# Attention on one core: the negated row maxima enter the transposed logits as a repeated stationary column times a unit matrix, and the values are split on ScalarE and VectorE

## The reference

```python
q, k, v = qkv(x)                                   # per image: 12 heads, 196 tokens, 16 channels
attn = einsum('bqd,bkd->bqk', q * scale, k)        # 196 x 196 per head
attn = attn + rel_h[..., :, None] + rel_w[..., None, :]   # bias from the query and the key's row and column
attn = softmax(attn, axis=-1)
out = einsum('bqk,bkd->bqd', attn, v) @ proj_w + proj_b
```

## Time and profile before

| | |
|---|---|
| three runs | 1793.18 us median (1792.56 to 1794.38) |
| the profiled execution, first to last instruction | span 1796.6 us |
| TensorE busy | 1485.9 us, 83% |
| VectorE busy | 1269.7 us, 71% |
| ScalarE busy | 973.4 us, 54% |
| GpSimd busy | 855.0 us, 48% |
| first layer's loop, reduce of step 0 to that of step 95 | 642.83 to 895.89 us |
| second layer's loop | 1483.92 to 1737.07 us |
| GpSimd busy in 850 to 900 us; in 1650 to 1700 us | 49.62 of 50; 49.48 of 50 |
| ScalarE's copy of the maxima (L1316), mean of 192 | 490 ns |
| granted TensorE clock, 700 to 900 us | 1.00 (full, 2.4 GHz) |

### The profile page before, as it was taken

One profiled execution on the slowest core, in us unless ns is written; L12 is line 12 of the kernel. 1 busy time (PEld: TensorE's weight loads), 2 busy tenths in 40 slices (PEclk: granted clock), 3 DMA queues, 4 the chain that ended last, 5 costly groups with the idle time before them and its releaser, 6 DMA issues. The chain is left out here.

```text
span 1796.6 us, 51708 instructions
## 1 busy us (share of the span) xinstructions
PE 1485.9 (83%) x19315; PEld 1272.1 (71%) x19315; DVE 1269.7 (71%) x4444; ACT 973.4 (54%) x1990; POOL 855.0 (48%) x1080
## 2 busy tenths in 40 slices
PE   4868888888876888889977999899998697888978
PEld 4757777777765776767755667678774586777766
DVE  7877787877778567879956684544446646888974
ACT  3633333333344567889924234555543556888972
POOL 2712222222235056879952111456551416787984
PEclk9955555555558889999986589899995798999998
DMA  3000000000002596667215204322225468666712
GB/s 87 1 20 4 4 5 4 4 4 4 4 3 83 171 257 151 147 156 161 58 48 173 98 24 151 125 81 86 83 73 153 144 159 254 166 147 150 146 29 58
DMA packets 72178, 165.21 MB, mean 92 GB/s; under 512 B 17938, under 2 KB 43162, under 8 KB 69436
## 3 DMA queue, kind: packets, MB, share of 16 engines
q1 hardware_dynamic: 66556, 149.05, 31.3%
q0 software_dynamic: 5376, 12.85, 2.3%
HBM read 93.84 MB, written 67.42 MB: 90 GB/s over the span
## 5 line engine op out<-in xcount | busy, mean ns | idle before, releaser
L1080 POOL TENSOR_TENSOR l_arena<-l_arena,l_arena 98x784 fp32r<-98x784 f32 x192 | 358.4, 1872 | 91.3 <-ACT l_arena L1328 79.0
L514 PE MATMUL gru_ps_r<-gru_hp,gru_wp 128*128 128x16 f16 x3920 | 200.1, 176 | 68.1 <-DVE gru_hp L489 68.1
L514 PEld LDWEIGHTS gru_ps_r<-gru_hp,gru_wp 128*128 128x128 f16 x3920 | 150.8, 106 | 88.5 <-DVE gru_hp L489 88.5
L567 POOL TENSOR_TENSOR gru_kept<-gru_keep,l0s_state 128x32 f32<-128x32 f32 x196 | 49.3, 251 | 305.4 <-ACT gru_keep L582 305.4
L1388 DVE TENSOR_REDUCE l_ps<-l_ps 98x4 f32<-98x784 f32 x192 | 187.5, 977 | 9.1 <-PE l_ps L1159 3.2
L514 PE MATMUL gru_ps_n<-gru_hp,gru_wp 128*128 128x16 f16 x3920 | 191.1, 174 | 0.0
L1197 PE MATMUL l_ps<-l_arena,l_arena 128*66 128x196 f32 x768 | 162.1, 264 | 20.9 <-POOL l_arena L1080 20.1
L580 ACT ACTIVATE gru_reset<-gru_ps_r,gru_unscale 128x32 f32<-128x32 f32 x196 | 56.4, 288 | 216.8 <-PE gru_ps_r L514 216.8
L1325 ACT ACTIVATE l_arena<-l_ps 98x784 fp32r<-98x784 f32 x192 | 158.4, 825 | 4.6
L1328 ACT ACTIVATE l_arena<-l_ps 98x784 f32<-98x784 f32 x192 | 157.0, 818 | 0.0
L1198 PE MATMUL l_ps<-l_arena,l_arena 128*66 128x196 f32 x768 | 155.0, 255 | 0.0
(11 more groups left out here) (389 smaller groups left out, 4568.9 us busy)
## 6 DMA issues: line engine op xcount, KB each, us to landing
l_arena<-qk SPq DMA_DIRECT2D x96, 294.0 KB
qk<-l_arena SPq DMA_DIRECT2D x48, 392.0 KB, 9.0
rel<-l_arena SPq DMA_DIRECT2D x24, 686.0 KB
l_arena<-rel SPq DMA_DIRECT2D x48, 343.0 KB
qk<-l_arena SPq DMA_DIRECT2D x12, 784.0 KB, 7.9
l_arena<-in_experts_dram SPq DMA_DIRECT2D x8, 1152.0 KB, 7.6
l_arena<-x SPq DMA_DIRECT2D x24, 294.0 KB, 5.3
l_arena<-x SPq DMA_DIRECT2D x24, 196.0 KB, 3.1
```

Source lines behind the costliest of these rows:

```text
L514: last = pe.matmul(out[:, b, B * m:B * m + B], wp[:, wi, g, m, :], hp[:, b, part, B * k:B * k + B], start=False, stop=True, skip_group_che ...
L1080: pool.tensor_tensor(pl[g % LOWS][:TH, :, :], p32[:TH, g % 2, :, :], ph[:TH, g % 4, :, :].bitcast(f32), ALU.subtract).then_inc(pl_ready, 1)
```

## The change

The maxima are no longer made into rows. VectorE's reduce writes the **negated** maxima straight into an SBUF tile `mt`, in one instruction. TensorE multiplies a stationary operand that is one column of `mt` repeated 98 times with a unit matrix repeated twice; the result, which has the negated maximum of each query in every row, is added in PSUM onto the transposed logits. I call these 4 matmuls **M**. X, its copy on ScalarE and the splitting of the maxima on VectorE are gone, as are the two rows in `q` and `k` and the fourth piece of each load. The splitting of the values leaves GpSimd: ScalarE rounds (`round_values`) after its exponentials, VectorE subtracts (`lower_values`) between its reduce and its keep, each in two of every four steps, and the first two groups ahead of the loop.

```diff
-ROWS = 106
-Q_ROWS, REL_ROWS = 2, 50
+ROWS = 104
+Q_ROWS, REL_ROWS = 0, 48
...
-    LOADS, SLOTS, LOWS = 4, 3, 3
+    LOADS, SLOTS, LOWS = 3, 3, 3
...
-        mt, ones_at = s.sb("mt", [128, 4, 2], bf16), s.sb("ones_at", [128, TH], bf16)
+        mt, unit = s.sb("mt", [128, 2, 4], f32r), s.sb("unit", [128, TH], f32r)
...
-                def split_values(n):
...
                 def logits_by_key(g):
                     b = g % B
-                    pe.wait_ge(x_copied, g + 1)
                     if g >= 2:
                         pe.wait_ge(p_ready, g - 1)
                     queries = slice(b * T, (b + 1) * T)
+                    both = unit[:TH, :].rearrange("p (a t) -> p a t", a=1).to_broadcast([TH, 2, TH])
                     for head in range(2):
+                        bank = ps[:TH, T_BANK + 2 * (g % 2) + head, :TB]
                         for half in range(2):
                             keys = slice(b * T + half * TH, b * T + (half + 1) * TH)
-                            last = pe.matmul(ps[:TH, T_BANK + 2 * (g % 2) + head, half * T:half * T + T], k[:, head, keys],
-                                             q[:, head, queries], start=True, stop=True)
+                            pe.matmul(bank[:, half * T:half * T + T], k[:, head, keys], q[:, head, queries],
+                                      start=half == 0, stop=False, skip_group_check=True)
+                    pe.wait_ge(max_ready, g + 1)
+                    for head in range(2):
+                        bank = ps[:TH, T_BANK + 2 * (g % 2) + head, :TB].rearrange("p (k t) -> p k t", k=2)
+                        for half in range(2):
+                            n = 2 * head + half
+                            last = pe.matmul(bank[:, :, half * TH:(half + 1) * TH], mt[:TH, g % 2, n:n + 1].to_broadcast([TH, TH]), both,
+                                             start=False, stop=half == 1, skip_group_check=True)
                     last.then_inc(t_summed, 1)
...
-                    if 1 <= i <= IMAGES:
-                        b = (i - 1) % B
-                        act.wait_ge(x_ready, i)
-                        act.activation(q[0:2, :, b * T:(b + 1) * T], ps[64:66, R_BANK, :TB].rearrange("p (h t) -> p h t", h=2), ACT.Copy).then_inc(x_copied, 1)
...
                         act.activation(p32[:TH, g % 2, :, :], banks, ACT.Exp).then_inc(p_ready, 1)
+                        n = g // 4 + 1
+                        if g >= 6 and n < IMAGES // 4 and g % 4 in (2, 3):
+                            act.wait_ge(o_summed, 4 * n - 4)
+                            round_values(n, g % 4 - 2)
...
+                def lower_values(n, head):
+                    dve.wait_ge(vh_ready, 2 * n + head + 1)
+                    dve.tensor_tensor(value_parts(n, head, 1), values_of(n, head), value_parts(n, head, 0).bitcast(f32), ALU.subtract).then_inc(vl_ready, 1)
...
                         dve.wait_ge(s_summed, i + 1)
-                        m = ps[:TH, S_BANK, 400:404]
-                        dve.tensor_reduce(m, ps[:TH, S_BANK:S_BANK + 2, :TB].rearrange("p c (h k) -> p c h k", h=2),
-                                          AXIS.X, ALU.max).then_inc(mx_ready, 1)
-                        dve.wait_ge(mx_ready, i + 1)
-                        if i >= 1:
-                            dve.wait_ge(x_ready, i)
-                        dve.tensor_copy(mt[:TH, :, 0], m).then_inc(mh_ready, 1)
-                        dve.wait_ge(mh_ready, i + 1)
-                        dve.tensor_tensor(mt[:TH, :, 1], m, mt[:TH, :, 0], ALU.subtract).then_inc(ml_ready, 1)
+                        if i >= 2:
+                            dve.wait_ge(t_summed, i - 1)
+                        dve.tensor_reduce(mt[:TH, i % 2, :], ps[:TH, S_BANK:S_BANK + 2, :TB].rearrange("p c (h k) -> p c h k", h=2),
+                                          AXIS.X, ALU.max, negate=True).then_inc(max_ready, 1)
+                    n = i // 4
+                    if 8 <= i < IMAGES and i % 4 in (2, 3):
+                        lower_values(n, i % 4 - 2)
```

More of the change, by code:

```diff
@@ L926, in load @@
                     rel = rel_dram[quad].rearrange("(g h r) c n -> g r c h n", g=2, h=2)[at].rearrange("r c h n -> (r c) h n")
-                    dst, row, src = ((q, Q_ROWS, qk[0]), (k, Q_ROWS, qk[1]), (q, REL_ROWS, rel), (q, 0, k[ROWS:ROWS + 2]))[piece]
-                    rows = 2 if piece == 3 else src.shape[0]
+                    dst, row, src = ((q, Q_ROWS, qk[0]), (k, Q_ROWS, qk[1]), (q, REL_ROWS, rel))[piece]
+                    rows = src.shape[0]
                     sp.dma_start(dst[row:row + rows, :, cols].bitcast(f32), src[:, :, cols].bitcast(f32)).then_inc(quarter_in[part], 16)
@@ L956, in main_step @@
                     p, b = divmod(i, B)
-                    part, piece = divmod(b - EACH - 1, LOADS)
-                    if i < IMAGES and p + 1 < PAIRS and part >= 0:
+                    part, piece = divmod(b - EACH - 1, EACH)
+                    if i < IMAGES and p + 1 < PAIRS and part >= 0 and piece < LOADS:
                         load(p + 1, part, piece)
-                    if i < IMAGES and p > 0 and part < 0:
-                        load(p, (b + B - EACH - 1) // LOADS, (b + B - EACH - 1) % LOADS)
+                    if i < IMAGES and p > 0 and part < 0 and piece < LOADS:
+                        load(p, part + PARTS, piece)
                     if i % 5 == 3 and i < 50:
@@ L1034, in _ @@
                 pool.wait_ge(q_padded, 1)
-                def split_values(n):
-                    p, part = divmod(n, 4)
-                    halves, slots = slice(8 * part, 8 * part + 8), slice(n % 2 * 8, n % 2 * 8 + 8)
-                    def whole(head):
-                        return v[:TH, halves, 32 * p + HD * head:32 * p + HD * head + HD]
-                    def place(head, low):
-                        at = 32 * head + HD * low
-                        return vs[:TH, slots, head, at:at + HD]
-                    def high(head):
-                        pool.tensor_copy(place(head, 0), whole(head)).then_inc(vh_ready, 1)
-                    def low(head):
-                        pool.wait_ge(vh_ready, 2 * n + head + 1)
-                        pool.tensor_tensor(place(head, 1), whole(head), place(head, 0).bitcast(f32), ALU.subtract).then_inc(vl_ready, 1)
-                    return high, low
                 def split_reciprocals(h):
@@ L1069, in _ @@
                 pool.wait_ge(pl_padded, LOWS)
-                for n in range(2):
-                    high, low = split_values(n)
-                    for head in range(2):
-                        high(head)
-                    for head in range(2):
-                        low(head)
                 for g in range(IMAGES):
@@ L1161, in logits_by_query @@
                     last.then_inc(s_summed, 1)
-                def maxima_to_rows(g):
-                    pe.wait_ge(ml_ready, g + 1)
-                    if g >= 1:
-                        pe.wait_ge(x_copied, g)
-                    for n in range(4):
-                        last = pe.matmul(ps[64:66, R_BANK, n * TH:n * TH + TH], mt[:TH, n, :], ones_at[:TH, :], start=True, stop=True)
-                    last.then_inc(x_ready, 1)
                 def logits_by_key(g):
                     b = g % B
-                    pe.wait_ge(x_copied, g + 1)
                     if g >= 2:
@@ L1299, in constants @@
                     act.wait_ge(const_in, 16)
-                    act.activation(ones_at[:TH, :], ident[:TH, :], ACT.Copy).then_inc(ident_ready, 1)
+                    act.activation(unit[:TH, :], ident[:TH, :], ACT.Copy).then_inc(ident_ready, 1)
                     act.wait_ge(pick_in, 16)
@@ L1311, in _, with round_values @@
                 last_order(item, value)
+                def round_values(n, head):
+                    act.activation(value_parts(n, head, 0), values_of(n, head), ACT.Copy).then_inc(vh_ready, 1)
+                act.wait_ge(ones_ready, 2)
+                for n in range(2):
+                    for head in range(2):
+                        round_values(n, head)
                 for i in range(IMAGES + 2):
-                    if 1 <= i <= IMAGES:
-                        b = (i - 1) % B
-                        act.wait_ge(x_ready, i)
-                        act.activation(q[0:2, :, b * T:(b + 1) * T], ps[64:66, R_BANK, :TB].rearrange("p (h t) -> p h t", h=2), ACT.Copy).then_inc(x_copied, 1)
                     if i >= 2:
@@ L1383, in _ @@
                 last_order(item, lambda i: None)
+                def lower_values(n, head):
+                    dve.wait_ge(vh_ready, 2 * n + head + 1)
+                    dve.tensor_tensor(value_parts(n, head, 1), values_of(n, head), value_parts(n, head, 0).bitcast(f32), ALU.subtract).then_inc(vl_ready, 1)
+                for n in range(2):
+                    for head in range(2):
+                        lower_values(n, head)
                 for i in range(IMAGES + LAG):
```

27 lines of the change are left out of this document (11 added, 16 removed).

## The result

The changed kernel takes **1782.43 us** (median of 9 runs, 1777.34 to 1790.41) where the kernel before takes 1792.56 (median of 9 beside it, 1784.84 to 1796.63). The ratio is 0.9946, with a 95% interval of 0.9928 to 0.9964: faster by 0.5%, about 10 us. The profiled execution of the changed kernel has a span of 1779.3 us.

The account below looks back on a forecast made before the run. GpSimd bounds A steps, VectorE's table-piece ring B and C steps. Per layer 4.1 (A) - 1.5 (C) - 1.4 (B) + 1.4 (ends) = 2.6 us, 5.2 for both: 1788 us, range 1772 to 1822.

Parts of the forecast that it names:

- the side that was given 0.47: Whole kernel: faster by over 0.2%, the summed forecast at 0.30 plus the rival without exclusion at 0.17.
- "1.98" for TensorE's own period: TensorE in an A step: AV 0.78, K 0.37, M 0.37 and Q 0.46 make 1.98 us.
- "2.15 against 2.22": A steps: 2.15 us each instead of 2.22, over 59 steps a gain of 4.1 us a layer.
- the 2.2 that I had named as a sign of being wrong: A steps: the forecast is wrong if they take above 2.2 us.
- L1365 due 1.01 after the start of its reduce: VectorE's value subtraction: due 1.01 us after its reduce starts, in A steps waiting 0.07 to 0.08 for GpSimd's pl.
- The exclusion: VectorE's L1365, with two SBUF inputs, waits until GpSimd's SBUF-reading pl ends; 0.28 us if it meets none.
- the first rival: L1365 arrives just after pl starts, waits 1.8 us more in eight A steps a layer; 1820 us, chance 0.33 in all.
- C steps, 0.6 for the first of two and nothing for the second: Steps 14, 46 and perhaps 43: L1365 delays keep and the ring 0.6 us, loss 1.5 us a layer.
- B steps, half of 2.8: Step pairs 34 and 38: L1365 behind pl makes keep 1.4 us late, 0 to 2.8 a layer, taken as 1.4.
- Ends of the loop, 1.4: Last item 0.8 us shorter and first exponential earlier by as much, against 0.2 for subtractions: 1.4 us a layer gained.
- No exclusion: L1365 takes 0.28 us whatever GpSimd does, no losses in B and C steps; 1775 us, chance 0.17.
- M slow: TensorE's M takes 0.88 us instead of 0.37, adding 15.0 us a layer in A steps; 1818 us, chance 0.07.

Follow-up runs that it names:

- the half that relieved the chain: Kernel before with only the new way of the maxima, the values still split on GpSimd; ratio 0.9888 to the kernel before.
- the half that relieved the busiest engine: Kernel before with only the value split moved from GpSimd to ScalarE and VectorE, maxima as before; alone, ratio 1.0239 to the kernel before.

## Why the prediction was right, and where its steps were not

The forecast was 1788 us, in a range of 1772 to 1822; the time is 1782.43, inside, on the side that was given 0.47. The mechanism held: GpSimd stops being the bound, M costs what K does, and L1365 takes part of the gain back by waiting for pl. The sum put 5.2 us where 10 were measured, and several of its terms were wrong in ways that cancel, so that the total came this near is in part luck.

- **A steps, "1.98" for TensorE's own period.** Mis-sized; the run with M doubled shows 1.83. I took Q to the next group as 0.46 from a step in which X followed Q; without X it is 0.37. AV was taken at 0.78 and is 0.73 when nothing interrupts it. So there was more room than I gave it.
- **A steps, "2.15 against 2.22", times 59.** The mean over all 59 is 2.13 and 2.10 in the two layers, near what I had, but from two parts that are both off. In the 31 late steps it is 2.03, a gain of 5.8 us where I had 2.2. In the other 28 it is 31.4 and 31.3 us per 14 in the first layer, 2.24 a step, which is above the 2.2 that I had named as a sign of being wrong, and no gain at all where I had 2. The loss sits in two steps of each 14, the one with a held L1365 and its echo; the other twelve take 2.06 each. An A step behind a C stretch is not a late one: L1365 of step 18 comes 0.51 after the start of pl. Without L1365 the same stretch takes 27.4. I had L1365 due 1.01 after the start of its reduce; it comes 0.89 after it, or 0.83.
- **The exclusion**, on which the first rival and the forecast both stood, is shown. Same place, same size, one operand from PSUM: never above 292 ns, against up to 1851. The Trainium skill's rule, "SBUF — State Buffer", section "Who interferes with whom", that a VectorE instruction with two SBUF inputs and a GpSimd one that reads SBUF exclude each other, agrees: two SBUF operands were held, one was not.
- **The first rival, late arrival,** given 0.33 and 1820 us. Its mechanism is real: in steps 18, 34 and 50, each behind a step with VectorE's reciprocal, L1365 comes 0.17 to 0.52 us after pl has started and is held for 1.2 to 1.6 us. But in the steps behind the other reciprocals (26, 42, 58, 66, 74, 82, 90) it takes 0.28 to 0.47, so the reciprocal alone doesn't do it. The three differ from these by the table piece in the step ahead; that this is the cause no run shows. I had counted eight losses among the A steps, and there were two, each about 1.4 us, with an echo of about 1.5 behind three of the four.
- **C steps, 0.6 for the first of two and nothing for the second.** The losses are 0.35 for the first (4.28 against 3.93) and nothing for the second, although it too is held (1.40 to 1.43 us long). **B steps, half of 2.8:** step 34 takes 4.13, where it took 2.74 before and 2.85 without L1365: a loss of 1.4 and 1.3; step 38 loses nothing. Taking half was the right size by chance, one of the two loses; the echo in step 35 came on top in one layer.
- **The echo** was in no case of mine: TensorE's pause of 1.58 us, and behind it matmuls at 0.37 instead of 0.25 at a granted clock of 0.52. A stall that I priced at its own length costs up to double.
- **Ends of the loop, 1.4.** The loss of X, its copy and VectorE's splits shortens every step in which the chain of an item is the bound, not only the last one: the first eight steps give 4.5 us. I costed the edit that removed them as if only the drain of the last item saw it. That drain, from the last reduce to the last keep, went from 9.92 and 10.23 us to 9.72 and 9.92, 0.2 to 0.3, where I had 0.8.
- **What was late next** in those steps I did not ask: the DMA store of the tables, which stood in no row of mine. ScalarE waits for it for 20.0 us in all instead of 4.8. Most of the 4.5 us is lost there, and the run that delays the loads gets a part back. That the loads are what slows the store down is the likeliest reading of that run, not proved: moving them also changes SyncE's queue ahead of the next store.
- **No exclusion** (1775 us) is excluded; **M slow** as well: by M doubled it is 0.37, the lower bound that I took. The 84 ns for 196 columns, which the prediction had from the Trainium skill, "TensorE: Matmul & The Clock Gate", section "Back-to-back issue gap", are there the gap of a matmul by itself, not of one in a stream; in this stream eight of M take 0.75 us, 94 ns each.

## What to carry to other kernels

Before a two-input VectorE instruction is put beside long GpSimd work, look at where in the step it falls: here 44 instructions of 0.28 us cost 10.8 us in the first layer, and the cure was another engine for the stretches in which they meet, or an operand in PSUM. Test the halves of a change separately: the half that relieved the chain was worth 1.1%, the half that relieved the busiest engine brought nothing on top, though the engine it relieved was 99% busy. And when the loop gets shorter, list what doesn't get faster with it, stores and loads first.

## What the runs showed of the hardware that I had not expected

- A stationary operand made of one column repeated 98 times, with a unit matrix read twice as the moving one, costs what a plain matmul of that shape does: 0.37 us for four, 250 ns at the shortest, 256 in the median.
- After a pause of 1.58 us TensorE's granted clock was 0.52 for the next 3 us, in 711 to 714. Behind the same step of the second layer it was not: the next step took 2.17. Over the two profiles of the changed kernel such an echo came in 7 of 12 places. What decides between the two no run here shows.
- The store of the tables landed, counted from the issue of its second half on SyncE to ScalarE's copy that waits for it, 10.3 and 10.2 us after it in the kernel before, 13.3 and 13.1 in the changed one (13.1 and 10.8 in its second profile), and 10.8 and 8.7 with the loads late. In step 43 the same stretch of time is 8.5 us in the kernel before and 8.5 to 8.6 in the changed one.
- An unchanged stretch of program, 576 to 588.5 us long, varied by 2% between profiles, which is more than the whole change. A difference under 1% can't be read from two spans.
